# Two newly written instruction orders, at the start and at the end of a fused attention and quantized-linear kernel

## The reference

```
x = x + attn(layernorm(x), wq, wk, wv, wo)      # 16 query heads, 4 key/value heads, head size 128
    scores = q k^T / sqrt(128), keys allowed: k <= q and (k < 4 or k >= q - 31)
    out = softmax(scores) v, then @ wo.T
x = x + ffn(layernorm(x), weight, bias)
    x_q = round(x / (max|x| / 127)) per row, w_q likewise per output, y = x_q w_q^T * scales + bias
```

## Time and profile before

| what | us |
|---|---|
| median of three timed runs (lowest, highest) | 616.41 (615.70, 616.91) |
| the profiled execution: its own time | 616.56 |
| its span in the trace | 614.8 |
| TensorE busy | 593.4 (97%) |
| VectorE busy | 544.4 (89%) |
| ScalarE busy | 394.6 (64%) |
| GpSimd busy | 337.3 (55%) |

### The profile page before, as it was taken

How to read it: one execution, slowest core, us unless ns; L and a number is a source line. 1 busy time by engine, 2 the same in 40 slices (tenths; PEclk the granted TensorE clock), 3 DMA queues, 4 the chain that set the end, 5 groups by cost and what they waited for, 6 DMA issues and landing times.

```text
span 614.8 us, 18062 instructions
## 1 busy us (share of the span) xinstructions
PE 593.4 (97%) x7566; PEld 523.8 (85%) x7566; DVE 544.4 (89%) x1072; ACT 394.6 (64%) x617; POOL 337.3 (55%) x320
## 2 busy tenths in 40 slices
PE   7699999999999999999999999999999999999994
PEld 6488878898888989889898988989898898989883
DVE  6999999898998989899898989979898897989886
ACT  6588646656656766665676666667666666765660
POOL 2667753564745556474555647455564645646563
PEclk8899999999999999999999999999999999999997
DMA  8565205060421506042160604316060421505001
GB/s 294 188 139 139 65 24 122 18 156 19 92 67 56 118 18 156 19 99 59 40 135 20 155 18 91 67 39 135 19 138 3 103 54 37 120 19 138 2 19 35
DMA packets 36272, 49.69 MB, mean 81 GB/s; under 512 B 2784, under 2 KB 22240, under 8 KB 36192
## 3 DMA queue, kind: packets, MB, share of 16 engines
q1 hardware_dynamic: 36048, 48.41, 31.9%
q10 hardware_dynamic: 144, 0.13, 0.1%
HBM read 35.42 MB, written 12.58 MB: 78 GB/s over the span
## 4 chain that ended last, share of the span: by engine, by line
PE 83%; DVE 11%; issue 2%; ACT 2%; POOL 2%; POOLq 0%; DVEq 0%; ACTq 0%
PE ps L436 24%; PE ps L557 23%; PE ps L466 8%; PE ps L404 6%; PE ps L415 6%; PE ps L510 4%; PE ps L540 4%; PE ps L539 4%; DVE Qs L1044 1%; DVE xn L1028 1%; PE ps L392 1%; PE ps L641 1%; PE ps L603 1%; DVE WqT L1182 1%; DVE sm L1062 1%
## 5 line engine op out<-in xcount | busy, mean ns | idle before, releaser
L436 PE MATMUL ps<-xT,WqT 128*128 128x256 f16 x1536 | 179.4, 273 | 2.2 <-DVE WqT L1182 1.4
L557 PE MATMUL ps<-WoT,pool 128*128 128x256 f16 x1440 | 167.3, 273 | 1.0 <-DVE pool L1071 1.0
L436 PEld LDWEIGHTS ps<-xT,WqT 128*128 128x128 f16 x1536 | 146.8, 98 | 19.0 <-DVE WqT L1182 1.8
L557 PEld LDWEIGHTS ps<-WoT,pool 128*128 128x128 f16 x1440 | 138.1, 98 | 16.3 <-DVE pool L1071 1.3
L1450 POOL TENSOR_TENSOR small<-E,rr 128x576 f32<-128x576 f32 x64 | 73.9, 1154 | 92.3 <-DVE rr L1066 92.3
L875 ACT ACTIVATE pool<-ps 128x512 f16<-128x512 f32 x128 | 69.9, 594 | 83.9 <-PE ps L540 83.8
L829 ACT ACTIVATE Qs<-ps 128x576 f16<-128x576 f32 x128 | 82.7, 646 | 44.4 <-PE ps L436 44.3
L1456 POOL TENSOR_TENSOR PP<-small,PP 128x576 f16<-128x576 f32 x64 | 82.2, 1284 | 50.3 <-ACT PP L865 50.3
L1439 POOL TENSOR_TENSOR Sm<-Sm,mx 128x576 f32<-128x576 f32 x64 | 74.9, 1170 | 46.2 <-DVE mx L1057 45.0
L1044 DVE TENSOR_TENSOR Qs<-ps,Qs 128x576 f16<-128x576 f32 x128 | 92.9, 727 | 4.5 <-ACT Qs L829 4.5
L1071 DVE SCALAR_TENSOR_TENSOR pool<-ps,pool 128x512 f16<-128x512 f32 x128 | 82.1, 680 | 0.0
(11 more groups left out here) (129 smaller groups left out, 913.7 us busy)
## 6 DMA issues: line engine op xcount, KB each, us to landing
values<-Vn SPq DMA_DIRECT2D x32, 256.0 KB, 2.0
VW<-values SPq DMA_DIRECT2D x16, 480.0 KB
big<-values SPq DMA_DIRECT2D x16, 480.0 KB
X<-in_L_attn_x SPq DMA_DIRECT2D x16, 256.0 KB, 8.4
VW<-values SPq DMA_DIRECT2D x16, 240.0 KB
big<-values SPq DMA_DIRECT2D x16, 240.0 KB
out<-pool SPq DMA_DIRECT2D x15, 256.0 KB, 6.0
big<-in_L_attn_wq SPq DMA_DIRECT2D x4, 512.0 KB, 8.7
```

Of the source, the lines that this page charges most:

```text
L436: a = pe.matmul(banks[BANK_Q[f]][:, j * 256:j * 256 + 256], WqT[:, k, wl, h * 128:h * 128 + 128], xT[:, b % 2, k, xl, :], start=(n == 1), ...
L557: a = pe.matmul(out_view(b, t), OT[:, p, ol, h, t * 128:t * 128 + 128], WoT[:, 4 * g + h, wl, :], start=first, stop=(end and g == KV - 1), ...
```

## The change

Four things, all in code that is written out by hand:

- **Weights.** GpSimd no longer squares wo nor makes low halves of weights. ScalarE squares the four quarters of wo with `weight_squares` (four columns of `am`, so that `scale_sums("o")` is four matmuls), and VectorE makes all low halves. `column_sums`, `column_copy`, `squares`, `weight_scaled`, GpSimd's `weight_low` and the tile `one` are gone.
- **The start of the queues.** The DMA of the float16 identity `idh` stands ahead of that of q0, and 8 more float32 matmuls on constants stand between TensorE's first `scale_sums` and `x_transpose(0)`.
- **Units 0 to 6** have new orders on all four engines.
- **Units 61 to 63** have new orders too. `out_last` can do two heads at a time, has a semaphore for each head and half, and does (2, 0), (3, 0), (2, 1), (3, 1) at the end, where it had (2, 0), (2, 1), (3, 0), (3, 1). `last_residual`, `last_quant` and `last_out` are cut into `last_residual`, `last_stats`, `last_norm`, `last_peak`, `last_scale`, `last_round`, `last_product` and `last_sum`, whose calls for the two halves are interleaved; the bias of each half is added behind its residual (`last_bias`).

The loop from unit 7 to unit 60 has the same instructions in the same order.

```diff
-            sp.dma_start(w_tile("q0"), wq_v[0]).then_inc(ld_q[0], 16)
             sp.dma_start(idh[:, :], idh_d).then_inc(ld_idh, 16)
+            sp.dma_start(w_tile("q0"), wq_v[0]).then_inc(ld_q[0], 16)
...
             scale_sums("k")
+            for _ in range(8):
+                pe.matmul(banks[BANK_S[0]][:, 0:128], small_ones[:, :], small_ones[:, :], start=True, stop=True)
             pe.wait_ge(ld_idh, 16)
...
-                act.activation(hi, src, ACT.Square, accum_out=am[:, SCALES[name]:SCALES[name] + 1]).then_inc(w_am[name], 1)
+                n, c = ("o", SCALES["o"] + int(name[1])) if name[0] == "o" else (name, SCALES[name])
+                act.activation(hi, src, ACT.Square, accum_out=am[:, c:c + 1]).then_inc(w_am[n], 1)
...
+            weight_squares("o0")
+            v_high(0, 1)
...
+            weight_squares("o1")
             exps(0)
-            k_high(0, 1)
-            weight_high("q3")
+            weight_squares("o2")
...
-            ln_norm(1)
-            exp_scale(1)
+            weight_low("v")
             k_low(0, 0)
...
-            weight_scaled("v")
-            weight_low("v")
-            squares("o0")
-            squares("o1")
+            ln_low(1)
             s_shift(0)
...
-            ffn_t(B - 2)
             out_last(3, 0)
-            ffn_mm(B - 2)
+            out_last(2, 1)
             out_last(3, 1)
-            ffn_last(0)
-            ffn_last(1)
+            ffn_t(B - 2)
+            ffn_mm(B - 2)
+            ffn_last_t(0)
+            ffn_last_mm(0)
+            ffn_last_t(1)
+            ffn_last_mm(1)
...
             last_residual(0)
+            last_stats(0)
+            last_norm(0)
+            last_residual(1)
+            last_stats(1)
+            last_peak(0)
+            last_scale(0)
+            last_norm(1)
+            last_peak(1)
+            last_round(0)
+            last_scale(1)
+            last_round(1)
             ffn_out(B - 2)
-            last_residual(1)
-            last_quant(0)
-            last_quant(1)
-            last_out(0)
-            last_out(1)
+            last_product(0)
+            last_product(1)
+            last_sum(0)
+            last_sum(1)
```

More of the change, by code:

```diff
@@ L80, in build @@
         diag = sb("diag", [128, 2, 128], F32)
-        am = sb("am", [128, 7], F32)
-        one = sb("one", [128, 2], BF16)
+        am = sb("am", [128, 10], F32)
         up = sb("up", [128, 7], F32)
@@ L148, in build @@
         ft_ps, fm_ps = sem("ft_ps"), sem("fm_ps")
+        out_last_ps = [[sem(f"out_last_ps{g}{t}") for t in range(2)] for g in range(KV)]
         ln_h = sem("ln_h")
@@ L182, in build @@
         w_l = {n: sem(f"w_l_{n}") for n in TILES}
-        w_c = {n: sem(f"w_c_{n}") for n in ("v", "o2", "o3")}
         def w_tile(name):
@@ L459, in scores @@
                         pe.wait_ge(k_l, 1)
-                    if c == 1 and u > 0:
+                    if c == 1 and 0 < u < NU - 2:
                         f_free(u - 1)
@@ L561, in out_proj, with out_last @@
                     a.then_inc(out_ps, 1)
-            def out_last(g, t):
+            def out_last(g, t, heads=range(4)):
                 u = NU - KV + g
@@ L569, in out_last @@
                     pe.wait_ge(f_x2, B - 1) if t == 0 else pe.wait_ge(s_m, NU)
-                for h in range(4):
+                for h in heads:
                     for n, (ol, wl) in enumerate(PAIRS):
@@ L651, in _ @@
             q_fill(0, 1)
+            v_fill(0, 0)
+            v_fill(0, 1)
+            scores(0)
             scale_sums("q2")
-            v_fill(0, 0)
-            scores(0)
-            v_fill(0, 1)
             q_fill(1, 0)
@@ L661, in _ @@
             k_fill(0, 1)
-            column_sums("o0")
             scores(1)
-            column_sums("o1")
-            column_sums("o2")
             q_fill(2, 0)
+            q_fill(2, 1)
+            q_fill(3, 0)
             x_transpose(1)
-            q_fill(2, 1)
+            scale_sums("o")
+            q_fill(3, 1)
+            p_transpose(0)
             pe.wait_ge(xt_ok, 2)
@@ L707, in _ @@
             scores(5)
-            pe.wait_ge(xt_ok, 3)
-            pe.wait_ge(k_l, 4)
-            k_fill(2, 0)
             out_proj(1)
-            q_fill(7, 0)
-            p_transpose(4)
-            pe.wait_ge(k_l, 5)
-            v_fill(2, 0)
-            scores(6)
             pv(3, 0)
@@ L720, in _ @@
             out_proj(2)
+            p_transpose(4)
+            q_fill(7, 0)
+            scores(6)
             pv(4, 0)
             pv(4, 1)
+            pe.wait_ge(k_l, 5)
+            v_fill(2, 0)
             out_proj(3)
@@ L872, in o_high @@
                 act.wait_ge(o_ps, 2 * u + j + 1)
-                if j == 0 and u > 1:
+                if j == 0 and u >= NU - 2:
+                    for t in range(2):
+                        act.wait_ge(out_last_ps[u - NU + 2][t], 1)
+                elif j == 0 and u > 1:
                     act.wait_ge(out_ps, u - 1)
@@ L912, in _ @@
[L912 to L930 removed]
+            k_high(1, 0)
@@ new lines, in _ @@
+            q_high(3, 1)
+            q_high(4, 0)
+            weight_high("o1")
+            p_high(1)
+            o_high(0, 0)
+            ln_split(2)
+            v_high(1, 0)
+            v_high(1, 1)
+            o_high(0, 1)
+            exps(2)
+            pt_evac(1)
+            q_high(4, 1)
+            k_high(1, 1)
+            p_high(2)
+            weight_high("o2")
+            x_evac(2)
+            exps(3)
+            pt_evac(2)
+            o_high(1, 0)
+            q_high(5, 0)
@@ L1246, in _ @@
             scale("q1")
-            ln_norm(1)
-            exp_scale(1)
+            weight_low("v")
             k_low(0, 0)
-            scale("q2")
             q_low(0, 0)
@@ L1253, in _ @@
             weight_low("q1")
+            v_low(0, 0)
+            ln_norm(1)
+            scale("q2")
             s_mask(0)
-            v_low(0, 0)
+            v_low(0, 1)
             s_peak(0)
+            scale("q3")
+            q_low(1, 0)
+            q_low(1, 1)
             weight_low("q2")
-            q_low(1, 0)
-            v_low(0, 1)
-            q_low(1, 1)
-            scale("q3")
+            weight_low("q3")
             probs(0)
             s_mask(1)
-            k_low(0, 1)
-            weight_low("q3")
             q_low(2, 0)
@@ L1351, in _ @@
                     ffn_norm(norm)
+                    ffn_peak(norm)
                 if quant is not None:
-                    ffn_quant(quant)
+                    ffn_scale(quant)
+                    ffn_round(quant)
                 if g == 0 and b + 2 < B:
```

461 lines of the change are left out of this document (207 added, 254 removed).

## The result

| | before | after |
|---|---|---|
| median of five timed runs (lowest, highest), us | 616.85 (615.70, 617.05) | 607.67 (606.61, 609.35) |
| ratio after/before, 95% interval | | 0.9856 [0.9844, 0.9867] |
| the profiled execution: its own time, its span | 616.56, 614.8 | 609.35, 607.5 |

The change makes the kernel 1.44% faster; 609.2 was predicted, which is 1.2%. Ratios here are of the means of the runs, so a gain in us is the ratio's distance from 1 times 616.6: 8.9 for the change. One thing has to be known before the profile is read: the profiled execution of the changed kernel is the slowest of its five, 1.7 us above the median, and experiments 4 and 6 show why.

The account below looks back on a forecast made before the run. TensorE was taken to bound the kernel, full in the loop, so only both ends could gain. 616.56 less 5.0 (start) and 2.3 (end) gave 609.3 for the profiled execution; predicted 609.2 us, range 605.8 to 612.4.

Parts of the forecast that it names:

- GpSimd in VectorE's way: Start: GpSimd's weight work stretches VectorE's instructions; batch 1's two xn take 3.65 us, forecast 0.73.
- To unit 7: Third unit's queries to scores(7): lay-out's 6.6 us lead cut by 1.6 for three collisions at 1.17 us each.
- lay-out: New instruction lists timed by predecessor and releaser, without new collisions: scores(7) at 81.0 us; start 6.6, end 2.5 gained.
- The start as a whole: Program start up to scores(7) at unit 7: gain of 5.0 us, bounds 6.6 and 2.7.
- The 8 matmuls: TensorE's start: eight extra constant matmuls cost 3.43 us and hold the transposes back until 10.3 us.
- The clock: TensorE's start: 2.4 GHz from 10 us on, k_fill 1.47 us not 2.72; clock worth 1.3 us by the first scores.
- first rival: Start: TensorE's gaps drop the clock again or ScalarE slips, so most gain is lost; 611.7 us, chance 0.12.
- Waits behind the first scores: Units 1 and 2: TensorE waits for query halves 1.5 us before the second scores, 0.4 behind, through ScalarE's gapless queue.
- The end: Units 61 to 63: two TensorE waits go, last projection ends at 602.0; gain 2.3 us, bounds 3.2 and 0.8.
- the lay-out holds whole: Rival, both ends: the full 6.6 us at the start and 2.5 at the end; 607.3 us, chance 0.15.
- VectorE becomes the bound: Rival, units 1 to 6: three low halves and their collisions make VectorE 5.0 us later; 619.1 us, chance 0.04.
- The end does not move: Rival, program end: VectorE's last chain eats TensorE's earlier finish, only the start counts; 611.4 us, chance 0.07.

Follow-up runs that it names:

- experiments 4 and 6: The runs pool_hold and bridge, in that order.
- pool_busy: Changed kernel, with GpSimd multiplying a spare tile six times where it did weight work before; 612.99 us, ratio 0.9941.
- start_only: Changed kernel's units 0 to 6 and weight work, with units 61 to 63 as before the change; 608.20 us, ratio 0.9874.
- pool_hold: Changed kernel, with GpSimd's add_product(13) waiting until VectorE has the scale of batch 14's norm; 606.69 us, ratio 0.9838.
- no_warm: Changed kernel without the 8 added float32 matmuls on constants; 608.61 us, ratio 0.987.
- few_squares: Against bridge: ScalarE squares one quarter of wo instead of four, and the scale comes from that quarter alone; 606.52 us, ratio 0.984.
- bridge: Changed kernel plus two runs of 5 constant matmuls where TensorE waits for ScalarE's squares at the start; 607.09 us, ratio 0.9848.
- bridge_hold: Changed kernel with both the added matmuls of bridge and the GpSimd wait of pool_hold; 606.31 us, ratio 0.9836.
- late_norm: Kernel before the change, with VectorE's normalization of batch 1 moved behind the last low half of unit 0's queries; 614.93 us, ratio 0.9975.
- best: Against bridge_hold: at the end, half 1's transposes precede half 0's matmuls and half 0's sum precedes half 1's product; 606.29 us, ratio 0.9836.

## Why the prediction was right in the sum, and where its steps failed

**What bounds it: right.** TensorE is full in the loop before and after, there is no wait in it, and what scores(7) gained the end kept.

**GpSimd in VectorE's way: right, and too small.** The prediction named the collision on `xn`, and `pool_busy` shows that GpSimd's absence is the larger part of the gain, 5.2 of 8.9 us, of which 0.9 is GpSimd's queue and not a collision. The step that failed is in "To unit 7": from the lay-out's 6.6 us it took 1.6 off, three collisions "at the price seen once", because softmax work on GpSimd would still meet the weight halves. None of the eight 128x1024 low halves met any: 1.27 to 1.29 us each. By the Trainium skill, SBUF — State Buffer, section "Who interferes with whom", the lock holds whole instructions and the first comer has it, and the prediction read that as a rule against this change. `pool_busy` agrees with the rule (2.38 us for a half-sized instruction that came 0.10 us late, and GpSimd's next ones held up in turn). The row that the prediction had for it was a weaker one: `xn` reads a single tensor from SBUF, while the low halves of `pool_busy` read two. But the rule did not speak against the change: neither side of the lock was held up by the moved low halves. GpSimd's weight instructions took 1.9 to 2.4 us, and they are gone; its softmax steps take 1.15 to 1.3, and the low halves fell into the idle time around them. That this would be so with other orders no run here shows.

**The start as a whole: 5.0 predicted, 7.8 measured** (`start_only`; the interval of the ratio makes it 6.6 to 8.9). The lay-out itself was too slow: it has scores(7) at 81.0, and where the clock holds they stand at 78.81 (`pool_hold`), 8.8 us before the 87.60 of the earlier trace rows. By then the third unit's first queries start at 26.18, 6.9 us earlier than before, where 5.3 were laid out; from there to scores(7) the rows gain 1.9 us, where the prediction had 1.3 and took 1.6 off. What the clock costs where it falls stands against this. In parts:

- *The 8 matmuls.* 3.43 us was the price, from 26 passes in 5.74. They took 2.03, 0.127 a pass and not 0.22, and the transposes begin at 8.68 and not at 10.3: GpSimd's low half of x (7.37 + 1.16 = 8.53) releases them, and the 8 are all but free (8.75 without them, in `no_warm`). The price was read from a stretch in which a pass took 0.22 us.
- *The clock.* "With no idle stretch ahead of it I expect 2.4 GHz": there were two, 1.23 and 0.97 us, which the prediction had in its first rival (gaps of 2.3 us of 3.8) and priced at 1.3, where the profiles show 2.5 at scores(7). The clock fell in the profiles of the changed kernel and of `start_only` and did not in that of `pool_hold`; the first scores, forecast near 20.0, begin at 21.69, 21.53 and 18.77. The 2.8 us between the last two are the clock's; in the changed kernel's profile weights that came late have a part, which the prediction did not have at all. By the Trainium skill, TensorE: Matmul & The Clock Gate, section "What's actually happening", how long a kernel runs cold differs from run to run with the phase of the chip's monitor at its start. `start_only` and `pool_hold` agree with it in that the same instructions, begun within 0.06 us of each other, take 1.83 and 1.47 us for the keys and 5.28 and 2.78 for the first queries. They differ in the place: here it is a clock that was up and fell again behind short waits. The monitor's phase no run here shows.
- *Waits behind the first scores.* 1.5 and 0.4 were laid out, 0.67, 0.32 and 0.72 measured (0.87 ahead of the second scores where the clock held): the size about right. The reason (ScalarE) is wrong for the waits behind the second scores, by `few_squares`; for the one ahead of them it stays open, as ScalarE and VectorE come within 0.03 us of each other there.

**The end: 2.3 predicted, 0.7 measured**; this is the step that failed worst. Of the prediction's "two waits go: 0.87 us ahead of the pair of `out_last` at 598.58", and "some 0.4 earlier", the smaller one went and the larger did not. The lay-out took the norm of batch 14 at 0.73 us, its length with GpSimd idle. But the change also drops GpSimd's wait ahead of `add_product(13)`, so that this addition and the bias run right beside that pair: 2.62 us, and TensorE waits 1.09. The prediction had looked for GpSimd's lock at the start, where it was being removed, and not at the end, where a wait that went brought it in. `pool_hold` puts it back and shows the price: 0.8 us in the pair `bridge` and `bridge_hold`. That is half of the 1.6 us that the term is off. For another part the lay-out had no source: it lets the last projection end 2.65 us earlier (604.65 - 602.0), and the terms that it names, 0.87, 0.4 and 0.65, make 1.9. The rest is open.

So 609.2 came near 607.7 by luck as well, by two errors that half cancel: 2.8 us too little for the start, 1.6 too much for the end. (The sum itself is 609.1, 616.41 - 7.3; the 609.2 comes of rounding on the way.) Of the rivals, "the lay-out holds whole" (607.3) was nearest in time, though not by its mechanism: it has 6.6 and 2.5, the runs 7.8 and 0.7. "VectorE becomes the bound" (619.1) stood on three collisions that did not occur. "The end does not move" was nearly true of the end. Open is how the 3.7 us that `pool_busy` leaves are shared between the new order, the clock and the column sums that went; `late_norm` gives 1.5 for one call's place while GpSimd works.

## What to carry to other kernels

Ask of every instruction on VectorE's critical stretch which GpSimd instruction can lie beside it, and price the collision at the rest of that instruction; to take long GpSimd work away was worth more than the waits it showed up as. When a change drops a wait on GpSimd, look at what now runs beside it: an operation that nobody waits for is better late than beside a norm on the path. And where a program's runs differ by more than others do, compare the clock of two profiles at the start; ten cheap matmuls in TensorE's waits cost nothing measurable here and took the spread from 2.7 to 0.2 us. Look also at when each profile's first weights landed, before all of such a difference is put down to the clock.

## What the runs showed of the hardware that was not expected

- The profile's granted clock reads 1.00 over the first 8 us in both kernels, yet constant matmul passes run at different speeds there: 26 of them in 5.74 us before and in 4.70 after (0.22 and 0.18 us each), and 16 in 2.03 behind them (0.13). The same 26 take 5.38 us in `pool_hold`. The granted-clock column does not tell TensorE's speed at the very start of a program; the passes do.
- The same start came out at either clock level, and the clock fell with no wait longer than 0.70 us between the transposes and the keys (`start_only`: keys from 11.18, granted clock 0.57 in the microsecond from 12, 1.00 again from 19; in `pool_hold`, keys from 11.12, it stayed at 1.00). It cost 2.5 us at unit 7 (scores(7) at 81.31 and 78.81).
- The same DMAs in the same order landed at different times: ScalarE's square of q0 starts at 9.22 us behind a wait of 0.63 for its weight in the changed kernel's profile, and at 8.59 without one in `pool_hold`'s.
- A collision costs about what is left of the other engine's instruction, whatever the size of one's own: a 128x512 low half paid 1.64 us and two 128x1024 ones 1.18 and 1.07, each 0.2 less than GpSimd's multiplication had left (`pool_busy`), and a 128x256 sum paid 0.84 where GpSimd's addition had 0.97 left (`best`). It goes both ways: GpSimd's multiplication took 2.75 us for 1.89 when it began beside a low half.
